# Two fp32 products of a graph-network kernel as fp32r products, VectorE's intermediates in PSUM, and new orders on four engines

## The reference

```python
x = _layernorm(x + _L0_gnn_ref(x, adj, ...))   # hypergraph convolution, twice, 512 hidden features
x = _layernorm(x + _L1_gnn_ref(x, adj, ...))   # relu([x, adj @ x / degree] @ W.T)
x = _layernorm(x + _L2_gnn_ref(x, adj, ...))   # three times adj @ (x @ W) + b, relu between
x = _layernorm(x + _L3_gnn_ref(x, adj, ...))   # relu((adj @ x) @ W)
```

```python
H = (adj != 0).astype(x.dtype)                 # incidence, 0 or 1
w = adj.reshape(N, -1)[:, :C]                  # weights: the first row of adj
Dn = jnp.einsum('nce,ne->nc', H, w)            # then 1 / Dn, or 0
Be = H.sum(axis=1)                             # then 1 / Be, or 0
m = Be[:, :, None] * jnp.einsum('nce,nch->neh', H, xw)
out = Dn[:, :, None] * jnp.einsum('nce,neh->nch', H, m)
```

## Time and profile before

| | value |
|---|---|
| Median of 3 runs | 1463.22 us (1462.11 to 1463.25) |
| The profiled execution's own time | 1463.48 us |
| Its span, first to last instruction | 1461.7 us |
| Mean granted TensorE clock | 0.991 |
| PE busy | 1416.2 us, 97% |
| PE weight loads busy | 1353.8 us, 93% |
| DVE busy | 1080.4 us, 74% |
| ACT busy | 1056.8 us, 72% |
| POOL busy | 851.7 us, 58% |
| Share of the 16 DMA engines' span | 9.8% in the kernel's queue |

### The profile page before, as it was taken

One profiled execution on the slowest core, in us unless ns is written; L12 is line 12 of the kernel. 1 busy time (PEld: TensorE's weight loads), 2 busy tenths in 40 slices (PEclk: granted clock), 3 DMA queues, 4 the chain that ended last, 5 costly groups with the idle time before them and its releaser, 6 DMA issues. The chain is left out here.

```text
span 1461.7 us, 33281 instructions
## 1 busy us (share of the span) xinstructions
PE 1416.2 (97%) x10896; PEld 1353.8 (93%) x10896; DVE 1080.4 (74%) x3744; ACT 1056.8 (72%) x2442; POOL 851.7 (58%) x776
## 2 busy tenths in 40 slices
PE   7899999999999999999999999999999999999974
PEld 6799999999999999999999999999999999999973
DVE  6667777777777777777777777777777777777663
ACT  4577777778777777777777777777777777777863
POOL 4565565565566566566566566566566566566542
PEclk9999999999999999999999999999999999999997
DMA  4001101101101101101101101101100100110000
GB/s 135 23 12 37 38 19 37 38 19 37 37 20 37 38 19 37 38 19 37 38 20 37 38 19 37 38 24 32 38 26 30 38 28 29 37 30 16 15 16 22
DMA packets 29946, 47.04 MB, mean 32 GB/s; under 512 B 3408, under 2 KB 12240, under 8 KB 29776
## 3 DMA queue, kind: packets, MB, share of 16 engines
q1 hardware_dynamic: 29776, 44.91, 9.8%
HBM read 28.12 MB, written 16.78 MB: 31 GB/s over the span
## 5 line engine op out<-in xcount | busy, mean ns | idle before, releaser
L1180 POOL TENSOR_TENSOR h_lo<-h_f,h_hi 128x512 fp32r<-128x512 f32 x128 | 166.2, 1298 | 373.4 <-ACT h_hi L541 373.4
L560 ACT ACTIVATE x<-n_s,n_shift,n_rstd 128x256 f32<-128x256 f32 x384 | 208.4, 590 | 101.0 <-DVE n_shift L832 101.0
L810 DVE BATCH_NORM_STATS2 n_st<-n_s 128x6 f32<-128x256 f32 x512 | 188.1, 409 | 7.6 <-POOL n_s L1254 5.2
L555 ACT ACTIVATE n_std<-n_mv,eps_c 128x2 f32<-128x2 f32 x256 | 74.7, 292 | 158.3 <-DVE n_mv L815 158.2
L1188 POOL TENSOR_TENSOR r_lo<-r_f,r_hi 128x512 fp32r<-128x512 f32 x128 | 163.5, 1299 | 36.6 <-ACT r_hi L541 36.4
L1246 POOL TENSOR_TENSOR n_s<-tk,mask 128x512 f32<-128x512 f32 x64 | 66.7, 1042 | 165.7 <-issue 150.4
L254 PE MATMUL psum<-v_hi,h_hi 128*128 128x256 f32 x512 | 148.9, 291 | 5.0 <-issue 5.0
L254 PE MATMUL psum<-A_f,x 128*128 128x128 f32 x1024 | 142.1, 282 | 5.4 <-ACT x L560 4.8
L254 PE MATMUL psum<-w2c_hi,r_hi 128*128 128x258 f32 x512 | 145.9, 285 | 0.5 <-POOL r_lo L1188 0.5
L254 PE MATMUL psum<-w2c_hi,r_lo 128*128 128x258 f32 x512 | 146.0, 285 | 0.0
L254 PE MATMUL psum<-w2c_lo,r_hi 128*128 128x258 f32 x512 | 144.8, 283 | 0.0
(11 more groups left out here) (141 smaller groups left out, 5044.1 us busy)
## 6 DMA issues: line engine op xcount, KB each, us to landing
x_in<-x_in_dram SPq DMA_DIRECT2D x64, 256.0 KB, 3.0
out<-x SPq DMA_DIRECT2D x64, 256.0 KB, 2.0
at_in<-adjT SPq DMA_DIRECT2D x64, 128.0 KB, 2.3
x<-v_in SPq DMA_DIRECT2D x3, 256.0 KB, 5.8
n_s<-w2T_in SPq DMA_DIRECT2D x2, 256.0 KB, 3.7
...
```

The lines of the kernel that those rows point to most:

```text
L555: act.activation(nm.std[:], nm.mv[:, :, 1], ACT.Sqrt, bias=eps_c[:, 0:1]).then_inc(nm.rooted, 1)
L560: last = act.activation(dst[:, g, :], nm.s[:, g, :], ACT.Identity, scale=nm.rstd[:, g:g + 1], bias=nm.shift[:, g:g + 1])
L810: last = dve.bn_stats(nm.st[:, g, :], nm.s[:, g, :])
L1180: return pool.tensor_tensor(dst[1][:], src, f(dst[0][:]), ALU.subtract).then_inc(signal, 1)
```

## The change

**Stage G.** `HT` and `BH` become fp32r. HT holds only 0 and 1. `BH` grows from 129 to 258 columns: 128 of HT times the rounded inverse `be_r`, 128 of HT times the rest `be_rest`, and the weight column as a rounded part and a rest. One fp32r matmul per graph takes the place of a plain one, with its output in a bank of its own for each graph (banks 5 and 7). The sum of the two halves is taken on DVE: a tensor_reduce for the degree, and `make_Gd` in three instructions where there was one. ACT gets `round_inverse`; POOL gets two instructions of 128x2 and a second one of 128x256 in `make_BH`.

**Stage GP.** `GT` and `p_f` are split into hi and lo (ACT `round_GT`, `round_p`; POOL `low_GT`, `low_p`), and GP becomes an fp32r `product`: six matmuls of 256 columns where there were two plain ones. It writes bank 4, and moves behind H2 in PE's order. It now waits for both parts of p and for GT's rest.

**PSUM.** `h_var`, the `mv` of n2 and n3, the two `agg` results and the sum of n1 are kept in PSUM. The `mv` of n1 and n4 stay in SBUF.

**Orders.** ACT computes `square_mean` and `root_h` ahead of the apply of n3, `round_p` behind it, and root n1, n2 and n4 elsewhere. DVE does G's scaling and the counts one after the other where they were interleaved, `make_p` ahead of the AXB chain, and n2's statistics right behind its sum.

```diff
-BANK = dict(R=0, Ax2=0, Tr=0, GP=0, H1=1, Gx=1, XAB=2, AXB=2, TK=2, H2=3, xT=4, P=4,
-            H2W=6, H1W=6, G=7, AP3=7, Ax3=7)
+BANK = dict(R=0, Ax2=0, Tr=0, GP=4, H1=1, Gx=1, XAB=2, AXB=2, TK=2, H2=3, xT=4, P=4,
+            H2W=6, H1W=6, G=(5, 7), AP3=7, Ax3=7)
...
-        HT = sb("HT", [2, C])
-        ht_count, be, be_inv = sb("ht_count", [2]), sb("be", [2]), sb("be_inv", [2])
-
-        BH = sb("BH", [2, C + 1])
+        HT = sb("HT", [2, C], F32R)
+        ht_count, be = sb("ht_count", [2]), sb("be", [2])
+        be_inv, be_r, be_rest = sb("be_inv", [2]), sb("be_r", [2], F32R), sb("be_rest", [2])
+
+        BH = sb("BH", [2, 2 * C + 2], F32R)
         dn_max, dn_inv, dinv = sb("dn_max", [2]), sb("dn_inv", [2]), sb("dinv", [2])
-        Gd = sb("Gd", [2, C])
+        Gl, Gd = sb("Gl", [2, C]), sb("Gd", [2, C])
         GT = [sb(f"GT{b}", [2, C]) for b in range(2)]
+        GT_s = [hi_lo(f"GT{b}", [2, C]) for b in range(2)]
...
+                self.st = sb(f"{name}_st", [2, 6])
+                if moments is None:
+                    self.mv = sb(f"{name}_mv", [2, 2])
+                else:
+                    self.mv = psum[:, moments, 0:4].rearrange("p (g t) -> p g t", g=2)
...
-        n1, n2, n3, n4 = Norm("n1"), Norm("n2"), Norm("n3"), Norm("n4")
+        n1, n2 = Norm("n1", sums=False), Norm("n2", moments=BANK["H1W"])
+        n3, n4 = Norm("n3", moments=BANK["AP3"]), Norm("n4")
...
-                pe.wait_ge(w_made, upto(p))
+                pe.wait_ge(w_lo, upto(p))
+                if begun(p - 2) and not first(n, 2):
+                    pe.wait_ge(p_made, upto(p - 2))
                 if begun(p - 5):
                     pe.wait_ge(ax3_lo, upto(p - 5))
                 for g in range(2):
-                    last = mm(psum[:, BANK["G"], g * (C + 1):(g + 1) * (C + 1)], HT[:, g, :], BH[:, g, :],
-                              True, True)
+                    last = mm(psum[:, bank("G", p)[g], 0:2 * C + 2], HT[:, g, :], BH[:, g, :], True, True)
                 last.then_inc(pe_did["G"], 1)
...
+                if not first(n, 2):
+                    pe.wait_ge(gd_made, upto(n))
...
             def GP(n, k):
                 p = n - 1
-                pe.wait_ge(p_made, upto(p))
-                if not first(n, 1):
-                    pe.wait_ge(gt_made, upto(n))
-                for g in range(2):
-                    last = mm(psum[:, bank("GP", p), g * D:(g + 1) * D], GT[(k - 1) % 2][:, g, :],
-                              p_f[:, g, :], True, True)
+                pe.wait_ge(p_hi, upto(p))
+                pe.wait_ge(p_lo, upto(p))
+                pe.wait_ge(gt_lo, upto(p))
+                for g in range(2):
+                    last = product(psum[:, bank("GP", p), g * D:(g + 1) * D],
+                                   [(part(GT_s[(k - 1) % 2], ALL, g), part(p_s, ALL, g))])
                 last.then_inc(pe_did["GP"], 1)
...
                 if active("Gx", n):
                     Gx(n, k)
+                if active("H2", n):
+                    H2(n, k)
                 if active("GP", n):
                     GP(n, k)
-                if active("H2", n):
-                    H2(n, k)
                 if active("TK", n):
                     TK(n, k)
...
+            def round_GT(n, k):
+                p = n
+                if begun(p - 2):
+                    act.wait_ge(pe_did["GP"], upto(p - 2))
+                copy(GT_s[k % 2][0][:].rearrange("p a b -> p (a b)"),
+                         psum[:, bank("Tr", p), 0:2 * C]).then_inc(gt_hi, 1)
+
+            def round_p(n, k):
+                p = n - 1
+                act.wait_ge(p_made, upto(p))
+                if begun(p - 1):
+                    act.wait_ge(pe_did["GP"], upto(p - 1))
+                copy(p_s[0][:], p_f[:]).then_inc(p_hi, 1)
...
+            def round_inverse(n, k):
+                q = n + 1
+                act.wait_ge(be_made, upto(q))
+                if begun(q - 1):
+                    act.wait_ge(bh_made, upto(q - 1))
+                copy(be_r[:], be_inv[:]).then_inc(be_hi, 1)
...
+                if active("prep", n):
+                    round_inverse(n, k)
                 if active("AP3", n):
                     p = n - 4
                     root(n3, p)
+                if active("P", n):
+                    square_mean(n, k)
+                    root_h(n, k)
+                if active("AP3", n):
+                    p = n - 4
                     if begun(p - 1):
                         act.wait_ge(pe_did["Ax3"], upto(p - 1))
                         act.wait_ge(n4.summed, upto(p - 1))
                         act.wait_ge(x3_nz, upto(p - 1))
                     apply(n3, p, x3)
-                if active("F", n):
-                    root(n4, n - 5)
-                if active("P", n):
-                    square_mean(n, k)
+                if active("GP", n):
+                    round_p(n, k)
                 if active("Tr", n):
                     copy_GT(n, k)
...
+                if active("Tr", n):
+                    round_GT(n, k)
+                if active("F", n):
+                    root(n4, n - 5)
...
+                dve.tensor_reduce(dn, out_G(n, 2 * C, 2 * C + 2), AX_X, ALU.add).then_inc(dn_0, 1)
+                dve.wait_ge(dn_0, upto(n))
...
-                dve.tensor_tensor(Gd[:], g_dn[:, :, 0:C], bc(dinv[:], [C, 2, C], 2), ALU.mult).then_inc(gd_made, 1)
+                dve.tensor_tensor(Gl[:], out_G(n, C, 2 * C), bc(dinv[:], [C, 2, C], 2), ALU.mult).then_inc(gl_made, 1)
+                dve.wait_ge(gl_made, upto(n))
+                for g in range(2):
+                    last = dve.scalar_tensor_tensor(out=Gd[:, g, :], in0=psum[:, bank("G", n)[g], 0:C],
+                                                    scalar=dinv[:, g:g + 1], in1=Gl[:, g, :],
+                                                    op0=ALU.mult, op1=ALU.add)
+                last.then_inc(gd_made, 1)
...
-                    last = dve.scalar_tensor_tensor(out=agg[:, g, :], in0=psum[:, BANK["AXB"] + g, 0:D],
+                    o = psum[:, BANK["AXB"] + g, 0:D]
+                    last = dve.scalar_tensor_tensor(out=o, in0=o,
                                                     scalar=rdeg[:, g:g + 1],
...
-                dve.scalar_tensor_tensor(out=n2.s[:], in0=agg[:], scalar=0.0, in1=x1[:],
+                dve.scalar_tensor_tensor(out=n2.s[:], in0=psum[:, BANK["AXB"]:BANK["AXB"] + 2, 0:D], scalar=0.0, in1=x1[:],
                                          op0=ALU.max, op1=ALU.add).then_inc(n2.summed, 1)
+
+            def moments_n2(n, k):
+                if first(n, 2):
+                    dve.wait_ge(gt_hi, upto(n))
+                if begun(n - 3):
+                    dve.wait_ge(h1w_out, upto(n - 3))
+                dve.wait_ge(n2.stats, upto(n - 2))
+                dve.memset(wait_pad[:], 0.0)
+                mean_var(n2)
...
                     shift(n3, n - 4)
                 if active("P", n):
                     wide_var(n, k)
+                if active("P", n):
+                    wide_invert(n, k)
+                    make_p(n, k)
                 if active("AXB", n):
                     node_degree_max(n, k)
+                    node_degree_recip(n, k)
+                    make_agg(n, k)
+                    sum_n2(n, k)
+                    stats(n2, n - 2)
                 if active("F", n):
                     invert(n4, n - 5)
-                if active("P", n):
-                    wide_invert(n, k)
+                    shift(n4, n - 5)
                 if active("AXB", n):
-                    node_degree_recip(n, k)
-                if active("F", n):
-                    shift(n4, n - 5)
-                if active("P", n):
-                    make_p(n, k)
-
-                if active("AXB", n):
-                    make_agg(n, k)
+                    moments_n2(n, k)
                 if active("Ax3", n):
                     dve.wait_ge(ax3_hi, upto(n - 4))
                     split_lo(ax3, flat(BANK["Ax3"]), ax3_lo)
-                if active("AXB", n):
-                    sum_n2(n, k)
                 if active("Gx", n):
                     split_gx(n, k)
+                if active("AXB", n):
+                    invert(n2, n - 2)
+                    shift(n2, n - 2)
                 if active("GP", n):
                     sum_n1(n, k)
-                if active("AXB", n):
-                    stats_alone(n2, n - 2)
-                if active("GP", n):
-                    stats(n1, n - 1)
-                if active("AXB", n):
-                    if active("GP", n):
-                        dve.wait_ge(n1.stats, upto(n - 1))
-                    invert(n2, n - 2)
-                elif active("GP", n):
-                    dve.wait_ge(n1.stats, upto(n - 1))
-                    dve.memset(wait_pad[:], 0.0)
-                if active("GP", n):
-                    mean_var(n1)
-                if active("AXB", n):
-                    shift(n2, n - 2)
```

(27 more changed lines are left out.)

153 lines of the change are left out of this document (80 added, 73 removed).

## The result

The changed kernel took 1506.97 us (median of 4 runs, 1506.82 to 1507.29), beside 1462.99 us for the kernel before on the same chip: ratio 1.0302, 95% interval 1.0284 to 1.0320. It is 44 us slower, where 1437 us had been forecast: rival (a) came true, in nearly every step of the loop.

A forecast was written before the change was run, and what follows sets the result against it. PE, busy 97% of the span, was taken to bound the kernel. G's and GP's savings of 28.9 us and 2 us of fill gave 1463.5 - 28.9 + 2 = 1436.6, so 1437 us; range 1430 to 1478.

The forecast's parts named there:

- rival (a): n4's shift on DVE loses the seam to POOL's x2c; PE waits 0.98 a step, 1497 us; chance 0.24, wholly or partly.
- the free case: n4's shift gets in at the seam between POOL's GT_lo and x2c and costs nothing.
- wins a seam: Argument from n3's shift: a waiting DVE instruction gets its turn between two POOL instructions, though POOL's next stands ready.
- So in the loop PE waits for nobody: PE in the loop before the change: longest wait 3.1 us, so each us cut from its stream shortens the step.
- G's saving: Stage G on PE: 0.45 now, 0.24 as two fp32r matmuls, 0.21 us saved in 61 steps.
- GP's saving: Stage GP on PE: 0.96 now, 0.70 as six fp32r matmuls, 0.26 us saved in 62 steps.
- the forecast's lower price: GP saves only 0.17 us, since some steps had it at 0.87; 23 us in all with G.
- H2 ahead of GP changes nothing in the number of switches: PE's new order of H2 and GP: no more switches between plain fp32 and fp32r, no cost given.
- rival (c): POOL makes p_lo late for GP beyond its 1.1 spare; all gain gone, 1463 to 1466 us; 0.07 together with rival (d).
- Spare 0.2: ax3_lo on DVE done at 19.74, TK's turn on PE at 19.95: the tightest place, if n4's shift takes 0.14.
- rival (b): Small waits at TK, Gx or XAB, or DVE late for h_var, cost 6 to 21 us: 1443 to 1458; chance 0.16.
- 2 us once: Fill: the longer way to GP and rounding of the inverse, uncovered in the first pairs; 2 us, bounds 0 and 6.

The follow-up runs named there:

- e7: The kernel before with one edit, n3's mean and variance placed in PSUM: 1446.18 us, ratio 0.9883.
- e8: The changed kernel with x2c ahead of xb on POOL, ACT's start-up rounding reordered, and ax3_lo directly behind n2's statistics on DVE: 1443.08 us.
- e2: The changed kernel with POOL's x2c put back ahead of xb, DVE untouched: 1452.91 us, ratio 0.9935.

## Why the prediction was wrong

**The step that failed** is the one at n4's shift: "The two starts come out within 0.02 us of each other ... I take the free case, narrowly". The mechanism, its place and its price (0.98, measured 0.90 to 0.95) were right and stood there as rival (a); x2c's start was right to 0.02. The request came 0.17 later than summed. The sum took most of the DVE instructions back to back; in the trace an instruction that needs the result of the one ahead begins behind its end: agg 0.10 after rdeg, n2_s 0.04 after agg, the statistics 0.04 after n2_s. With such gaps the chain came to 0.17 more. The argument that a waiting DVE "wins a seam" needs DVE to wait when the seam comes; 0.21 behind x2c's start it did not yet, and GT_lo to x2c left no room. By the Trainium skill, SBUF — State Buffer, section "Who interferes with whom", issue order decides who blocks; the rows agree: x2c issued first, and the shift took 1.10.

**"So in the loop PE waits for nobody"** was wrong too. e7 shows that 0.28 a step of it was short waits under the matmuls' records, for x3 and for p_f. One part of the change, n3's moments in PSUM, is worth all of that, and the forecast had no term for it on PE.

**G's saving**, 0.21, was right (0.24 in place of 0.45).

**GP's saving**, 0.26, was mis-sized: the 0.96 that it started from held 0.10 that belongs to the wait (0.86 in e7), and the new one costs 0.79 and not 0.70. From e7 to e8 GP loses 0.07 and TK 0.10, together the forecast's lower price, 0.17. H2, now ahead of GP, gains 0.07 (0.81 to 0.88). "H2 ahead of GP changes nothing in the number of switches" may stand, but the forecast did not ask what H2 waits for in its new place, and it is n2's sum. The net is 0.10.

**What must keep up.** p_lo was in time for GP in the loop (721.59, GP at 722.57), and p_f and GT were too: rival (c) did not happen. "Spare 0.2" for ax3_lo at TK was not there: with the hold gone (e2) TK waits for it, and the step is 0.20 above e8's. That is rival (b), under (a). With that wait gone too, the step is 21.33, against 21.36 forecast. That it is so near is luck, the right sum from wrong terms: 21.84 - 0.28 - 0.21 - 0.10 is 21.25, and the other stages' slots are some 0.08 longer in e8 than in e7, 0.02 of it R.

**Start and end.** "2 us once" for the start was 5.7, near its bound of 6; POOL's queue (p_lo behind a BH that waits for ACT) was overlooked. The end had no term, and cost 1.8.

The range's top, 1478, left (a) in full outside, with 0.24 for (a) as a whole. A tie within the error of the sum, with 60 us on one side, should have had near even chances, and then the range has to reach beyond 1497. Even (a)'s own price was 10 us short: with the hold the step was 22.44 where 21.36 + 0.98 = 22.34 was forecast, and start and end took 5.5 us more.
